# Routing weights of a mixture of experts broadcast by DMA, the shared expert taken first, and three PSUM banks each for gate and up

## What is computed

```python
x = x + 0.5 * ffn(layernorm(x))        # "FFN 1", k = 1 in the kernel
x = x + mixer(layernorm(x))            # gated convolution, scan over time, output product, layer norm
x = x + 0.5 * ffn(layernorm(x))        # "FFN 4", same weights, k = 4

def ffn(tokens):                       # E = 32 experts of width I = 64, plus a shared one of width 128
    idx, w = route(tokens)             # sigmoid scores, 2 of 4 groups, 4 experts; weights sum to 2.5
    gate = silu(einsum('th,eih->tei', tokens, gate_w))
    up   = einsum('th,eih->tei', tokens, up_w)
    y    = einsum('tei,ehi->teh', gate * up, down_w)
    mixed  = (take_along_axis(y, idx[:, :, None], 1) * w[:, :, None]).sum(1)
    shared = (silu(tokens @ sh_gate.T) * (tokens @ sh_up.T)) @ sh_down.T
    return mixed + shared
```

## Time and profile before

| | |
|---|---|
| median of 3 runs | 806.41 us (805.25 to 808.37) |
| profiled execution, first to last instruction | 805.2 us |
| PE matmul busy | 745.0 us, 93% |
| DVE busy | 660.7 us, 82% |
| POOL busy | 451.7 us, 56% |
| ACT busy | 416.5 us, 52% |
| DMA | 10.53 MB, mean 13 GB/s, nearly all in the first 20 us |
| granted TensorE clock, mean | 0.975 |

### The profile page before, as it was taken

The page is one execution under the profiler, slowest core; times in us unless marked ns, Lnnn a source line. Parts: engine busy times, 40 slices in busy tenths (PEclk is TensorE's granted clock), DMA queues, the critical chain, the costliest instruction groups (busy, mean ns, idle before and its releaser), DMA issues. The chain is left out here.

```text
span 805.2 us, 12283 instructions
## 1 busy us (share of the span) xinstructions
PE 745.0 (93%) x3320; PEld 586.7 (73%) x3320; DVE 660.7 (82%) x1719; ACT 416.5 (52%) x777; POOL 451.7 (56%) x444
## 2 busy tenths in 40 slices
PE   6799967999999999999999999999999999978897
PEld 5577745777878678777778678786778678756685
DVE  5887767698889979898889988898888988876863
ACT  4445534455555456564555456564655455453453
POOL 3245644456755567556755576465855576554364
PEclk9799989899999999999999999999999999998999
DMA  8100000000000000000000000000000000000000
GB/s 203 35 0 1 14 0 1 26 1 0 15 1 27 2 1 13 26 0 1 13 0 26 0 1 13 0 26 1 13 0 13 0 0 14 1 0 1 0 14 13
DMA packets 22867, 10.53 MB, mean 13 GB/s; under 512 B 5376, under 2 KB 22816, under 8 KB 22816
## 3 DMA queue, kind: packets, MB, share of 16 engines
q1 hardware_dynamic: 22288, 9.74, 4.5%
q10 hardware_dynamic: 528, 0.26, 0.1%
HBM read 7.90 MB, written 2.10 MB: 12 GB/s over the span
## 5 line engine op out<-in xcount | busy, mean ns | idle before, releaser
L398 POOL TENSOR_TENSOR hid_lo<-hid,hid_hi 128x512 fp32r<-128x512 f32 x272 | 355.5, 1308 | 281.2 <-ACT hid_hi L514 280.7
L514 ACT ACTIVATE hid_hi<-hid 128x512 fp32r<-128x512 f32 x272 | 171.1, 629 | 198.1 <-DVE hid L667 175.2
L652 DVE TENSOR_TENSOR weighted<-silu_sb,wb_ps 128x512 f32<-128x512 f32 x256 | 174.2, 681 | 75.5 <-ACT silu_sb L505 48.4
L505 ACT ACTIVATE silu_sb<-gate_ps 128x512 f32<-128x512 f32 x272 | 160.6, 591 | 111.8 <-PE gate_ps L940 110.5
L667 DVE TENSOR_TENSOR hid<-weighted,up_ps 128x512 f32<-128x512 f32 x256 | 174.2, 680 | 13.8 <-DVE weighted L652 1.7
L938 PE MATMUL up_ps<-xT_hi,wt_hi 128*128 128x512 f32 x238 | 99.6, 419 | 17.7 <-DVE hid L667 17.4
L1003 PE MATMUL down_ps<-hid_lo,wt_hi 128*128 128x512 f32 x272 | 108.8, 400 | 3.2 <-POOL hid_lo L398 3.2
L1000 PE MATMUL down_ps<-hid_hi,wt_hi 128*128 128x512 f32 x272 | 109.5, 403 | 2.4 <-ACT hid_hi L514 2.4
L1001 PE MATMUL down_ps<-hid_hi,wt_lo 128*128 128x512 f32 x272 | 108.3, 398 | 0.0
L960 PE MATMUL wb_ps<-wT,pick 128*128 128x512 f32 x256 | 101.0, 405 | 1.5 <-DVE weighted L652 1.5
L938 PE MATMUL gate_ps<-xT_hi,wt_hi 128*128 128x512 f32 x238 | 100.1, 421 | 2.5 <-issue 2.5
(11 more groups left out here) (150 smaller groups left out, 1105.5 us busy)
## 6 DMA issues: line engine op xcount, KB each, us to landing
x_res<-in_L_attn_x SPq DMA_DIRECT2D x8, 256.0 KB, 2.9
out_x<-x SPq DMA_DIRECT2D x8, 256.0 KB, 2.3
x_ln<-in_L_attn_x SPq DMA_DIRECT2D x7, 256.0 KB, 3.0
raw<-in_L_ffn_gate_w SPq DMA_DIRECT2D x4, 256.0 KB, 5.4
raw<-in_L_ffn_up_w SPq DMA_DIRECT2D x4, 256.0 KB, 5.0
raw<-in_L_ffn_down_w SPq DMA_DIRECT2D x4, 256.0 KB, 5.4
x_ln<-in_L_attn_x ACTq DMA_DIRECT2D x1, 256.0 KB, 5.4
raw<-in_L_attn_W_in SPq DMA_DIRECT2D x1, 128.0 KB, 2.8
```

What stands on the lines that cost most here:

```text
L398: nc.gpsimd.tensor_tensor(hid_lo[s][:, :], hid[s][:, :], hid_hi[s][:, :].bitcast(F32), ALU.subtract).then_inc(hid_lo_done, 1)
L505: nc.scalar.activation(silu_sb[s][:, :], gate_ps[s][:, :], ACT.Silu).then_inc(silu_done, 1)
L514: nc.scalar.activation(hid_hi[s][:, :], hid[s][:, :], ACT.Copy).then_inc(hid_hi_done, 1)
L652: V.tensor_tensor(weighted[s][:, :], silu_sb[s][:, :], wb_ps[j % 2][:, :], ALU.mult)\
```

## The change

- The pick matmuls, `pick` and the `wb_ps` banks go. Routing weights are kept in one float32 copy (`w_tok` as (expert, block of 128 tokens) columns), so that one transposition does for four, and part 10 of the routing loses its last two DVE instructions. The result is stored to HBM (`wT_hbm`, 64 KB), and SP reads it back, each expert's row 64 times, into `wb`, which lies in the space of `raw`: 16 pairs x 128 partitions x 2 KB = 4.2 MB for each unit, as four chunks of 2, 4, 5 and 5 pairs of two DMAs each. `weigh_tile` reads `wb` from SBUF.
- The transposition of the weights moves from slot 0 of the unit that uses them to slot 14 (unit (4,i-1), for the next FFN 1) or 15 (unit (1,i), for the next FFN 4) of the unit before, with the ACT copy. Routing parts 8 and 9 of PREPARE move from slots 13.5 and 14 to 9.5 and 12.5, part 10 from 14.5 to 13.5; in TAIL parts 3 to 10 move up to end at 14.5 instead of 15.5.
- The shared expert is tile 0, so tiles 1 to 16 are weighed.
- Three banks for gate and three for up (`BANKS = 3`): gate waits for `weighted`, up for `hid` of the tile three before. The silu is written over the gate in PSUM; only tile 0's goes to SBUF.
- SP: each unit's store and read-back stand between the loads of x; `load_x_ln(i + 2)` comes behind the read-back for unit (1,i+1).

```diff
+BANKS = 3
...
+def pair_tile(q):
+    return 4 + 12 * (q // 4) + q % 4
...
-    return gate_tile(j) + (4 if j < NPAIR else 1)
+    return gate_tile(j) + (4 if j else 1)
...
+CHUNKS = ((0, 2), (2, 6), (6, 11), (11, 16))
...
         PREPARE = {"transpose 1": 1, "xT high 1": 1, "xT low 1": 1.5, "router 1": 2, "logits 1": 2.5,
-                   "silu logits 1": 3, "route 1": (4.5, 5, 5.5, 6, 6.5, 8.5, 9, 9.5, 13.5, 14, 14.5)}
+                   "silu logits 1": 3, "route 1": (4.5, 5, 5.5, 6, 6.5, 8, 8.5, 9, 9.5, 12.5, 13.5),
+                   "weights 1": 14}
...
-                "route 4": (10.5, 11, 11.5, 12, 12.5, 13, 13.5, 14, 14.5, 15, 15.5)}
+                "route 4": (10.5, 11, 11.5, 11.5, 12, 12.5, 13, 13.5, 14, 14.5, 14.5), "weights 4": 15}
...
-                "route 4": (13.5, 13.5, 14, 14.5, 15, 15.5, 15.5, 16.5, 16.5, 16.5, 16.5)}
+                "route 4": (13.5, 13.5, 14, 14.5, 15, 15.5, 15.5, 16.5, 16.5, 16.5, 16.5), "weights 4": 17}
...
+                 "route 1": (6.5, 7, 8, 8.5, 9, 9.5, 10, 10.5, 11, 12, 13), "weights 1": 14}
...
+            def broadcast_weights(k, b):
+                sp.wait_ge(wT_done[k], b + 1)
+                if is_first(k, b):
+                    sp.wait_ge(w_transposed, NBATCH)
+                else:
+                    for loaded in wb_loaded:
+                        sp.wait_ge(loaded, ffns_before(k, b) * 32)
+                sp.dma_start(wT_hbm.rearrange("e (t p) -> (e t) p", t=TT), wT[k][:, :]).then_inc(wT_stored, 16)
+                sp.wait_ge(wT_stored, ffns_before(k, b) * 16 + 16)
+                for c, (lo, hi) in enumerate(CHUNKS):
+                    if not is_first(k, b):
+                        sp.wait_ge(weighted_done, first_pair(k, b) - NPAIR + hi)
+                    for half in range(2):
+                        rows = wT_hbm.rearrange("(q h) t -> h q t", h=2)[half, lo:hi, :]
+                        sp.dma_start(wb[half * I:half * I + I, lo:hi, :], rows.partition_broadcast(I))\
+                          .then_inc(wb_loaded[c], 16)
...
+            broadcast_weights(1, 0)
             load_x_ln(2)
+            broadcast_weights(1, 1)
             load_x_res(1)
-            with sp.Fori(2, NBLK - 1) as i:
+            broadcast_weights(4, 0)
+            broadcast_weights(1, 2)
+            for i in range(2, NBLK - 1):
                 load_x_res(i)
                 load_x_ln(i + 1)
                 store(i - 2)
+                broadcast_weights(4, i - 1)
+                broadcast_weights(1, i + 1)
             load_x_res(NBLK - 1)
-            for b in range(NBLK - 3, NBLK):
-                store(b)
+            store(NBLK - 3)
+            broadcast_weights(4, NBLK - 2)
+            broadcast_weights(4, NBLK - 1)
+            store(NBLK - 2)
+            store(NBLK - 1)
...
-                s = (start_parity(k, b) + j) % 2
+                s = j % BANKS
                 act.wait_ge(gate_ready, n + 1)
-                if not (isinstance(n, int) and n < 2):
-                    act.wait_ge(hid_done, n - 1)
-                nc.scalar.activation(silu_sb[s][:, :], gate_ps[s][:, :], ACT.Silu).then_inc(silu_done, 1)
+                if j == 0 and not is_first(k, b):
+                    act.wait_ge(hid_done, n - NT + 1)
+                nc.scalar.activation(gate_ps[s][:, :] if j else silu_sb[:, :], gate_ps[s][:, :], ACT.Silu)\
+                  .then_inc(silu_done, 1)
...
             def wT_copy(k, b):
                 act.wait_ge(route_transposed[k], b + 1)
-                nc.scalar.activation(wT[k][:, :], side[:, :], ACT.Copy).then_inc(wT_done[k], 1)
+                if not is_first(k, b):
+                    act.wait_ge(wT_stored, ffns_before(k, b) * 16)
+                nc.scalar.activation(wT[k][:, :], side[:, 0:P], ACT.Copy).then_inc(wT_done[k], 1)
...
             def weigh_tile(k, b, j):
                 n = first_tile(k, b) + j
-                s = (start_parity(k, b) + j) % 2
                 dve.wait_ge(silu_done, n + 1)
-                dve.wait_ge(wb_ready, first_pair(k, b) + j + 1)
-                V.tensor_tensor(weighted[s][:, :], silu_sb[s][:, :], wb_ps[j % 2][:, :], ALU.mult)\
+                dve.wait_ge(wb_loaded[chunk_of(j - 1)], ffns_before(k, b) * 32 + 32)
+                V.tensor_tensor(weighted[j % 2][:, :], gate_ps[j % BANKS][:, :], wb[:, j - 1, :], ALU.mult)\
                  .then_inc(weighted_done, 1)
...
-                    st.done(V.scalar_tensor_tensor(weight[:, :, :], chosen[:, :, :], SCALE,
+                    st.done(V.scalar_tensor_tensor(w_tok[:, :, :].rearrange("p e t -> p t e"), chosen[:, :, :], SCALE,
                                                    winv[:, :].unsqueeze(2).broadcast_to([P, TT, E]),
                                                    ALU.mult, ALU.mult))
-                    st.wait()
-                    st.done(V.tensor_copy(w_tok[:, :, 0:E], weight[:, :, :]))
-                    st.wait()
-                    st.done(V.tensor_tensor(w_tok[:, :, E:2 * E], weight[:, :, :], w_tok[:, :, 0:E].bitcast(F32),
-                                            ALU.subtract))
...
+            def bank_free(k, b, j):
+                before = j - bank_before(j)
+                if before == 0:
+                    pe.wait_ge(silu_done, first_tile(k, b) + 1)
+                elif before > 0:
+                    pe.wait_ge(weighted_done, first_pair(k, b) + before)
+                elif not is_first(k, b):
+                    pe.wait_ge(weighted_done, first_pair(k, b) - NPAIR + before + NT)
             def up_tiles(k, b, j):
                 n = first_tile(k, b) + j
-                s = (start_parity(k, b) + j) % 2
-                late = not (isinstance(n, int) and n < 2)
-                if late:
-                    pe.wait_ge(silu_done, n - 1)
+                s = j % BANKS
                 g, u = gate_tile(j), up_tile(j)
+                bank_free(k, b, j)
                 product(gate_ps[s][:, :], wt_hi[:, g, :], hi_of(k, b), lo_of(k, b), wt_lo[:, g, :],
                         True, True).then_inc(gate_ready, 1)
-                if j == 1:
-                    pe.wait_ge(wT_done[k], b + 1)
-                    spread_weights(k, b, 0)
-                if 0 < j < NPAIR:
-                    spread_weights(k, b, j)
-                if late:
-                    pe.wait_ge(hid_done, n - 1)
+                last = n - bank_before(j)
+                if not (isinstance(last, int) and last < 0):
+                    pe.wait_ge(hid_done, last + 1)
...
             def transpose_route(k, b):
                 pe.wait_ge(route[k], b * ROUTE + ROUTE)
-                transpose4(lambda t: w_tok[:, t, :].bitcast(F32), route_transposed[k])
+                nc.tensor.transpose(side[:, 0:P], w_tok[:, :, :].rearrange("p e t -> p (e t)"), ident[:, :])\
+                  .then_inc(route_transposed[k], 1)
...
-                    if j == 0:
-                        if "weights" in free:
-                            pe.wait_ge(*free["weights"])
-                        transpose_route(*main)
                     if j < LAG and before is not None:
                         for last in (((0, 1), (2,), ()) if slots > NT else ((0,), (1,), (2,)))[j]:
                             down(*before, NT - LAG + last)
                     if LAG <= j < NT + LAG:
                         down(*main, j - LAG)
+                    if j == steps.get("weights 1"):
+                        if "weights 1" in free:
+                            pe.wait_ge(*free["weights 1"])
+                        transpose_route(1, prepare)
+                    if j == steps.get("weights 4"):
+                        transpose_route(4, tail)
...
-                return {"weights": (res_done, i), "transpose ffn 4": (wT_done[1], i + 1),
+                return {"transpose ffn 4": (res_done, i),
                         "transpose 4": (halved_done, i - 1)}
             def free_second(i):
-                return {"mixer out": (mix_val_done, i + 1), "transpose 1": (wT_done[4], i),
+                return {"weights 1": (mix_val_done, i + 1), "mixer out": (wT_done[1], i + 2),
+                        "transpose 1": (wT_done[4], i),
```

More of the change, by code:

```diff
@@ L41, with chunk_of @@
 RING = 3
+BANKS = 3
 NBATCH = 14
+def pair_tile(q):
+    return 4 + 12 * (q // 4) + q % 4
+SHARED = 52
 def gate_tile(j):
-    return 4 + 12 * (j // 4) + j % 4 if j < NPAIR else 52
+    return pair_tile(j - 1) if j else SHARED
 def up_tile(j):
-    return gate_tile(j) + (4 if j < NPAIR else 1)
+    return gate_tile(j) + (4 if j else 1)
 def down_tile(j):
-    return gate_tile(j) + (8 if j < NPAIR else 2)
+    return gate_tile(j) + (8 if j else 2)
+CHUNKS = ((0, 2), (2, 6), (6, 11), (11, 16))
+def chunk_of(q):
+    return next(c for c, (lo, hi) in enumerate(CHUNKS) if lo <= q < hi)
 WIN_G, WIN_V, WOUT, WROUTER = 0, 1, 2, 3
@@ L90, in sem @@
             return ctx.enter_context(nc.semaphore(name))
-        gate_ps = [psum("gate_ps0"), psum("gate_ps1")]
-        up_ps = [psum("up_ps0"), psum("up_ps1")]
```

(22 more changed lines are left out.)

44 lines of the change are left out of this document (21 added, 23 removed).

## The result

The changed kernel takes 862.03 us (median of 4 runs, 860.52 to 865.69), the kernel before 807.39 on the same chip: a ratio of 1.0698, 95% interval 1.0671 to 1.0725. It is 7% slower. Its profiled execution spans 859.7 us against 805.2.

What follows compares the result with a forecast made beforehand. DVE was taken to bound most of a pair, PE and routing only the joints: 805.2 + 13.2 (steady pairs) + 16.8 + 5.4 (slow clock) - 2.6 (start, end, long units) = 838 us, range 782 to 866.

Steps and rivals of the forecast that it cites:

- the side that had 0.68: Whole kernel: the chance given to the change making it slower by more than about 0.5%, 4 us.
- its own mechanism: Joints between units: PE waits in order for routing and its clock falls; 838 us, bounds 820 to 860, chance 0.40.
- a pair near 97 us: Sign in the profile after: a pair of units takes near 97 us under this forecast, before 91.4.
- DVE sets the pace: DVE paces some 65 of 91 us of a pair; PE and routing set it only at joints between units.
- PE's wait in order: Before transposing the weights, PE waits for routing's end: 4.8 to 5.8 us at one joint, 2.3 to 3.7 at the other.
- the first joint: Unit (4,i-1) to (1,i+1), wait in slot 14: +1.4 us a pair, before any loss by a slow clock.
- R: End of routing part 10 on DVE, from which the prediction counts PE's work and the weights' store and read.
- the second joint: Unit (1,i) to (4,i-1), wait in slot 15: +1.2 us a pair, with the weights' store and read setting the end.
- The DMA path: Transposition and copy 0.7 us, store 2.3, two 256 KB reads 2.9 and 1.1 more: weights at R + 7.0.
- The clock: PE at 1.2 GHz for 6.5 us after long waits: +16.8 us at first joints, +5.4 at every other second one.
- Rival 3: Reads too slow: under about 200 GB/s DVE stops for x_ln in slot 8; 874 us at 150 GB/s, chance 0.12.
- The edges: Start, end and the two long units: -6.0 and +3.4, together -2.6 us, bounds -12 to +8.

Runs made afterwards that it cites:

- the filled wait: 18 unused 512-column matmuls on PE ahead of its wait for the transposition in units of 17 slots, against the changed kernel: 844.3 us, ratio 1.0473.

## Why the prediction was right, and where its sum was short

838 was forecast, 862 measured, inside the range of 782 to 866, on the side that had 0.68. But 862 lies above the 820 to 860 that the prediction gave its own mechanism, and 4 us below the range's upper end: its mechanism is there and costs 39 us, and another 15 that it did not have fit into a range made wide for its rivals. That they fit was luck. Of its signs, PE's waits and the slow clock behind them came; a pair near 97 us did not (100.6 to 102.6; 95.5 with DVE's loop written out).

**DVE sets the pace.** Right. PE was relieved of 256 matmuls and no pair got shorter; only the stretch behind the last pair did, by 1.9 us. DVE's work in a pair fell by 0.6 to 0.8 us (forecast 1.0), its idle time rose from 10.7 us to between 20.5 and 22.7.

**PE's wait in order.** Right at the first joint: 5.0 us (forecast 4.8 to 5.8). At the second it was 5.2 and not 3.7. There DVE wrote w_tok in 1.27 us instead of 0.39, which accounts for 0.9 of the 1.5. The trace has one difference between the two: in all six writes of 1.27 us a `hid_lo` of POOL had begun 0.24 us before and was still running, in the ten of 0.38 to 0.39 us no instruction of POOL was. No run moved one without the other. DVE's two products for tile 1 of unit (1,i+1) ended, with its loop written out, at 394.34, with R = 381.93: R + 12.4, where the working said 11.0, or 13.8 with the slow clock. At the second joint of the changed kernel the product that waited for the read started at 349.18, R + 7.4, against 7.0.

**The DMA path.** The store landed after 1.6 us, not 2.3, and the first 256 KB read after 3.9, not 2.9: two errors that cancel. The Trainium skill ("DMA: Bandwidth & Descriptors", the anatomy of one DMA) has a fit, for DMAs that GpSimd issues, that gave 2.2 us for the store and R + 6.1 for the whole path; the trace does not agree, with 1.6 and R + 7.4.

**The clock.** Right in kind: 0.50 behind both waits. In the three pairs it lasted 9.4, 5.9 and 3.0 us behind the wait of the first joint (forecast 6.5), and 3.0, 2.9 and 3.7 behind that of the second, where the prediction counted it at every other one and it came at each. Forecast for this was 16.8 + 5.4 = 22.2, and the filled wait is worth 17.7, net of the reads.

**Rival 3.** The reads did move at 210 to 231 GB/s, above the 200 from which it decides; x_ln was issued at 398.1 and lands 16.2 later in the median, R + 27.7 (forecast R + 26), and no wait for it shows in the pairs. The Trainium skill ("Advanced Engine Details and Errata", DMA Bandwidth Details) gives 27.2 GB/s for a port, 218 for eight; by that rule, the trace agrees in the mean (219 GB/s from 392 to 410), though single stretches reach 231, and no run wrote another number of partitions.

**The missing term.** This is the step that failed. The sum priced what the reads do to the instructions that wait for data, and not what they do to an engine that waits for its own code: DVE's jump back stood in it at nothing. With DVE's loop written out in both kernels the change costs 840.7 - 801.5 = 39.2 us; the sum said 32.8. With the loops it costs 54.6. The difference, some 16 us (21.3 gained in the one, 4.1 to 4.8 in the other), is the stop at DVE's loop end, grown by the reads from under 2 us to over 7 at four jumps, with PE's second slow stage. That is two thirds of the error of 24.

**The edges.** The rest is a term of the wrong sign. Compared store by store, with the loops written out, the first out_x goes out at 219.2 instead of 211.8, five pairs take 4.8 to 5.1 more (forecast 5.9), the sixth, which contains unit (4,6) and its wait for y_lo, 9.7 more, and the end is 1.6 shorter. So start and end are +5.8, not -2.6: PE waits for w_tok 16 times, and not in the six pairs alone. The slow clock is the larger part of it: with the wait filled as well, the first out_x goes at 214.5, so 4.7 of the 7.5 are gone. What the rest of it and the long sixth pair are made of, no run separates.

**The margins of the parts.** Moved routing +75 alone. With the slow clock and the stop dealt with, 822.1 against 801.5 remain, 20.6 us: PE's wait itself, which still holds tile 15 back, and the reads, which no run tells apart.

## What to carry to other kernels

An in-order wait can cost TensorE its clock too: filling it with useless work gave back 17.7 of 55 us here. Before a large transfer is put beside a loop, look at where each engine's loop ends: a jump back over a long body had to load code, and here that took over 7 us beside 4.2 MB of reads; writing the one loop out brought 21 us, and 0.5% even without the reads. Where a stop has no cause in the view of waits, the packets of the instruction queues can have it. And count what moves forward so that a transfer can be hidden, since here the moves alone cost more than the whole change.

## What was not expected of the hardware

- DVE stood 7.1 to 7.5 us at its loop's end with DMA at 213 to 226 GB/s, 1.8 to 1.9 us with a quarter of the bytes, 1.6 to 1.9 us in the kernel before with the shared expert first, and not at all without the loop. The 8 KB instruction packet started 4.6 to 5.0 us after the stop began in the first case, and up to 0.4 us before it in the second.
- The silu took 581 ns written over its own PSUM bank and 591 ns written to SBUF. The product took 685 ns with its weights in SBUF and 681 with them in PSUM.
- PE waits of nearly equal length (six of 5.1 us in the mean, 5.2 the longest) were followed by 2.9 to 9.4 us at a granted clock of 0.50. What sets that length was not tried.
- The same write of w_tok by DVE (128x128 in float32) took 0.39 us, and 1.27 us in each of the cases where a GpSimd tensor_tensor was running when it began.
